# Attention on eight cores: statistics taken inside the projection loop, scores and value products issued in another order

## What is computed

```python
# attention: 16 heads of 64, latent 128, 32 "rope" columns a head
q = rms_norm((x @ Wq) per head, q_g)
kv = x @ Wkv                      # 128 latent columns
k = rms_norm((kv @ Wk) per head, k_g)      # 32 columns a head
v_c = (kv @ Wv) per head                   # 32 columns a head
scores = einsum('bhtr,bhsr->bhts', q[..., :ROPE], k) / sqrt(HD)
probs = softmax(where(causal, -inf, scores))
out = einsum('bhts,bhsd->bhtd', probs, v_c), padded to 64 columns a head
attn = out @ Wo
# linear layer: blocks of 32 of xn and of the weight rounded to a 6-bit grid
ffn = xd @ wd.T + bias
return x + attn + ffn
```

## Time and profile before

| what | value |
|---|---|
| median of 2 runs | 5157.03 us (5156.27 to 5157.78) |
| the profiled execution | 5152.05 us |
| its span, slowest core (7) | 5150.5 us |
| spans of the 8 cores | 5126.5 to 5150.5 us |
| PE busy | 3178.5 us (62%) |
| DVE busy | 1221.0 us (24%) |
| ACT busy | 603.1 us (12%) |
| DMA | 101.99 MB, mean 20 GB/s |

### The profile page before, as it was taken

How to read it: one execution, slowest core, us unless ns; L and a number is a source line. 1 busy time by engine, 2 the same in 40 slices (tenths; PEclk the granted TensorE clock), 3 DMA queues, 4 the chain that set the end, 5 groups by cost and what they waited for, 6 DMA issues and landing times.

```text
span 5150.5 us, 61902 instructions; the slowest of 8 cores (5126.5 to 5150.5 us)
## 1 busy us (share of the span) xinstructions
PE 3178.5 (62%) x26106; PEld 2348.7 (46%) x26106; DVE 1221.0 (24%) x2264; ACT 603.1 (12%) x587; POOL 85.2 (2%) x164
## 2 busy tenths in 40 slices
PE   0455577777411354667777776777776776763777
PEld 0333355555300121224666665465662664453777
DVE  7322211111377667621000000100002000113000
ACT  0000000000000000001333332133330332120000
POOL 0000000000000000000000000000000000001111
PEclk6555677777655667786877777687776887675998
DMA  4111200000000010000000000000000000000222
GB/s 121 53 37 37 66 9 13 13 13 13 13 17 16 12 33 17 33 25 1 1 1 1 1 1 1 1 1 1 1 1 0 1 1 1 17 22 5 62 65 63
DMA packets 50904, 101.99 MB, mean 20 GB/s; under 512 B 8582, under 2 KB 26822, under 8 KB 50632
## 3 DMA queue, kind: packets, MB, share of 16 engines
q1 hardware_dynamic: 45512, 89.50, 5.5%
q0 software_dynamic: 5120, 8.53, 0.7%
HBM read 81.09 MB, written 16.78 MB: 19 GB/s over the span
## 4 chain that ended last, share of the span: by engine, by line
PE 57%; DVE 20%; issue 11%; ACT 7%; DMA 3%; SPq 1%; DVEq 1%; POOL 0%; ACTq 0%; POOLq 0%
PE psA L151 31%; PE psB L151 21%; ACT arena L911 6%; PE psA L156 5%; DMA arena<-xown 2%; DVE arena L503 1%; SPq L144 1%; DVEq L108 1%; DVE arena L396 1%; DVE arena L394 1%; DVE arena L735 1%; DVE arena L595 1%; DMA arena<-arena 1%; DVE arena L858 1%; DVE arena L399 1%
## 5 line engine op out<-in xcount | busy, mean ns | idle before, releaser
L151 PE MATMUL psA<-arena 32*128 32x128 f32 (+5 forms) x15616 | 1625.5, 331 | 343.6 <-DVE arena L983 103.5
L151 PE MATMUL psB<-arena 128*64 128x128 f32 (+3 forms) x9814 | 1297.9, 384 | 671.0 <-ACT arena L911 504.2
L151 PEld LDWEIGHTS psA<-arena 32*128 32x128 f32 (+4 forms) x15616 | 1325.5, 225 | 672.6 <-issue 639.4
L151 PEld LDWEIGHTS psB<-arena 128*64 128x64 f32 (+3 forms) x9814 | 918.1, 188 | 996.3 <-issue 981.8
L156 PE MATMUL psA<-arena 128*128 128x128 f32 (+1 forms) x608 | 264.0, 434 | 909.5 <-DVE arena L384 460.8
L911 ACT ACTIVATE arena<-psA,arena 128x1024 f32<-128x1024 f32 x544 | 580.0, 1111 | 1587.1 <-PE psA L151 1587.1
L156 PEld LDWEIGHTS psA<-arena 128*128 128x128 f32 (+1 forms) x608 | 106.8, 176 | 1067.6 <-issue 1067.6
L943 DVE TENSOR_TENSOR arena<-psB,arena 128x1024 f32<-128x1024 f32 x24 | 29.4, 1225 | 1046.5 <-PE psB L151 1046.5
L939 DVE COPY arena<-psB 128x1024 f32<-128x1024 f32 x16 | 19.6, 1225 | 777.7 <-PE psB L151 777.7
L625 ACT ACTIVATE arena<-psB,arena 16x128 f32<-16x128 f32 x16 | 5.8, 360 | 1191.5 <-PE psB L151 1191.5
L820 ACT ACTIVATE arena<-psA,arena 16x1024 f32<-16x1024 f32 x4 | 4.4, 1107 | 1062.9 <-PE psA L151 1062.9
(11 more groups left out here) (84 smaller groups left out, 914.4 us busy)
## 6 DMA issues: line engine op xcount, KB each, us to landing
arena<-xb SPq DMA_DIRECT2D x64, 512.0 KB, 3.4
arena<-xown SPq DMA_DIRECT2D x48, 512.0 KB, 4.7
out<-arena SPq DMA_DIRECT2D x32, 256.0 KB, 2.3
arena<-out POOLq DMA_DIRECT2D x128, 64.0 KB, 2.7
out<-arena SPq DMA_DIRECT2D x128, 64.0 KB, 2.0
arena<-wq SPq DMA_DIRECT2D x8, 512.0 KB, 8.5
arena<-fw SPq DMA_DIRECT2D x8, 512.0 KB, 3.4
arena<-wop SPq DMA_DIRECT2D x8, 512.0 KB, 7.2
```

Source lines behind the costliest of these rows:

```text
L151: lambda e: e.matmul(out, lhsT, rhs, start=start, stop=stop, tile_position=tp, skip_group_check=skipg),
```

## The change

Two edits that share nothing. **In stage A** the separate statistics pass is gone: the projection loop now loads each tile once, into one of four buffers instead of two (`abufs`), and takes its sums and its mean and inverse root at once, on one column, before the projection of the same tile. **In stage D** the 16 score matmuls are issued bank by bank (r outside, j inside) instead of going round the banks, and the AV matmuls take first the eight heads whose probabilities are in the first exponential (0, 1, 4, 5, 8, 9, 12, 13), then the other eight.

```diff
--- before.py
+++ after.py
@@ -473,22 +473,44 @@
             t_cskv = dve(lambda e: e.tensor_copy(cskv(), bank(6, 0, LAT, 0, 1)),
                          waits=[tmm])
 
-            tuse = [None, None]
-            t_st = stats(w, dx, NT, tuse)
-            t_fin = stat_finish(w, NT, t_st)
-
-            tuse = [t_fin, t_fin]
+            abufs = [tmt(0), tmt(1), xet(0), xet(1)]
+            tuse4 = [None] * 4
             t_kv_prev = None
+            t_fin = None
             for it in range(NT):
-                bi = it % 2
-                t_l = dma("sync", tmt(bi)[:], dx[128 * it:128 * it + 128, :],
-                          waits=[tuse[bi]])
+                bi = it % 4
+                t_l = dma("sync", abufs[bi][:], dx[128 * it:128 * it + 128, :],
+                          waits=list(tuse4[bi] or ()))
+                t1 = dve(lambda e, it=it, bi=bi: e.reduce_sum(
+                    stc(0, it), abufs[bi][:], AX), waits=[t_l])
+                t2 = dve(lambda e, bi=bi: e.tensor_tensor(
+                    qs(3), abufs[bi][:], abufs[bi][:], OP.mult), waits=[t1])
+                t3 = dve(lambda e, it=it: e.tensor_reduce(
+                    stc(1, it), qs(3), AX, OP.add), waits=[t2])
+                tf = dve(lambda e, it=it: e.tensor_scalar(
+                    stc(2, it), stc(0, it), 1.0 / 1024, None, OP.mult),
+                    waits=[t3])
+                tf = dve(lambda e, it=it: e.tensor_tensor(
+                    qs(2, 0, 1), stc(2, it), stc(2, it), OP.mult), waits=[tf])
+                tf = dve(lambda e, it=it: e.scalar_tensor_tensor(
+                    qs(2, 64, 1), stc(1, it), 1.0 / 1024, qs(2, 0, 1),
+                    OP.mult, OP.subtract), waits=[tf])
+                tf = act(lambda e: e.activation(qs(2, 0, 1), qs(2, 64, 1),
+                                                AF.Ln, bias=epsln(), scale=1.0),
+                         waits=[tf, t_eps])
+                tf = act(lambda e, it=it: e.activation(stc(3, it), qs(2, 0, 1),
+                                                       AF.Exp, bias=zcol(),
+                                                       scale=-0.5),
+                         waits=[tf, t_z])
+                tf = dve(lambda e, it=it: e.tensor_scalar(
+                    stc(0, it), stc(2, it), -1.0, None, OP.mult), waits=[tf])
+                t_fin = tf
                 tpm = pet(bank(3, 0, 128, 0, 1), stc(0, it), idt(),
-                          waits=[t_fin, w.tok("dv")])
+                          waits=[tf, w.tok("dv")])
                 t_evm = dve(lambda e: e.tensor_copy(mrow(), bank(3, 0, 128, 0, 1)),
                             waits=[tpm])
                 tpa = pet(bank(6, 0, 128, 0, 1), stc(3, it), idt(),
-                          waits=[t_fin, w.tok("dv")])
+                          waits=[tf, w.tok("dv")])
                 t_eva = dve(lambda e: e.tensor_copy(arow(), bank(6, 0, 128, 0, 1)),
                             waits=[tpa])
                 tra = mm(bank(7, 0, 128), onesr(128), arow(), True, True,
@@ -496,10 +518,12 @@
                 t_ar = dve(lambda e: e.tensor_copy(areps(), bank(7, 0, 128)),
                            waits=[tra])
                 t_ev = []
+                pe_last = None
                 for ci in range(8):
                     tp = pet(bank(ci // 4, 128 * (ci % 4), 128),
-                             tmt(bi)[:, 128 * ci:128 * ci + 128], idt(),
+                             abufs[bi][:, 128 * ci:128 * ci + 128], idt(),
                              waits=[t_l, w.tok("dv")])
+                    pe_last = tp
                     t_ev.append(dve(lambda e, ci=ci: e.tensor_copy(
                         xfms(ci), bank(ci // 4, 128 * (ci % 4), 128)), waits=[tp]))
                 for ci in range(8):
@@ -512,7 +536,7 @@
                     kvf(128, 128 * it), bank(2, 0, 128),
                     areps()[0:LAT, :], OP.mult), waits=[tmm, t_ar])
                 t_kv_prev = t_kv
-                tuse[bi] = t_kv
+                tuse4[bi] = (t_kv, pe_last)
             t_kv_done = w.tok("dv")
 
             if stop_after == "A":
@@ -880,8 +904,10 @@
                         continue
                     av_started = {}
                     av_last = {}
+                    av_order = ([h for h in range(16) if h % 4 < 2] +
+                                [h for h in range(16) if h % 4 >= 2])
                     for st in range(lo, hi):
-                        for head in range(16):
+                        for head in av_order:
                             av_last[((head // 2) // 4, 64 * (head % 2))] = (st, head)
                     t_avmm = None
                     for st in range(lo, hi):
@@ -890,8 +916,9 @@
                         pcnt[0] += 1
                         t_exp = [None, None]
                         lastb = [None] * 4
-                        for h in range(16):
-                            r, j = h % 4, h // 4
+                        for r in range(4):
+                          for j in range(4):
+                            h = 4 * j + r
                             lastb[r] = mm(
                                 setap2(r, 128 * j, 128),
                                 khat(h // 4, 128 * (st - sup * spt), 128)[32 * r:32 * r + 32, :],
```

## The result

| | before | changed |
|---|---|---|
| median | 5152.49 us (10 runs, 5145.44 to 5197.6) | 4975.49 us (11 runs, 4970.83 to 5121.05) |
| profiled execution | 5152.05 us, span 5150.5 | 4973.29 us, span 4971.8 |
| ratio | | 0.9657, 95% interval 0.9625 to 0.9688 |

The changed kernel is faster by 177 us, where 457 were forecast. Single executions of any of these kernels are now and then some per cent longer; the ratios leave them out, so a ratio is not the quotient of two medians.

The account below looks back on a forecast made before the run. Attention's steps were taken as bound by a chain of waits, with more lost to the half clock. 5152 - 520 (stage D) + 64 (stage A) = 4696, median 4700 us; range 4630 to 5350, the forecast's own 4630 to 4780.

Parts of the forecast that it names:

- the AV order: Stage D steps: eight AV heads fill the second wait, saving 0.75 us a step; plain 4.55 us, masked 7.23, together -532.
- the half clock: Stage D: a few stretches after a slot begins run at reduced clock, so -520 us is taken instead of -532.
- stage A: Token tile loop: statistics moved into the projection pass cost +64 us, between +50 and +85, with a 20.3 us period.
- the chain: Stage A: the small statistics operations run once per tile, 32 times at 1.90 us, net +59 us.
- the clock of the kv matmuls: Stage A: longer TensorE idling may slow the nine kv matmuls per tile; up to 20 us, taken as 5.
- the cost of the score order: Stage D: the 16 scores issued bank by bank still take 1.24 us a step, not 3.74; the order changes nothing.
- rival 3: Stage D scores: TensorE reaches only two or three quarters; scores 1.9 to 2.4 us, 4730 to 4950; 0.17 shared with another rival.
- Rival 1: Stage D scores: matmuls start only after those ahead have started; 3.04 us a step, kernel slower at 5340 us; chance 0.17.
- rivals 1 and 2: Stage D scores queue: 5340 us with some overlap (0.17); with none and a sinking clock, 5600 or beyond 6300 (0.08).
- the clock: Stage D: shorter steps and less idling put all steps at the full clock, 1.00, instead of a mean of 0.75.

Follow-up runs that it names:

- the blocks of two: The changed kernel with scores issued two matmuls per row quarter, then two of the next, instead of bank by bank: 4702.58 us, ratio 0.9136.
- the filler: The changed kernel with two unread 128-row matmuls added per step between the scores and the first AV: 4918.23 us, ratio 0.9549.

## Why the prediction was right and wrong

**Right: the AV order.** Forecast 4.55 us a plain step and 7.23 a masked one, 1323 us for all; with the AV order alone 4.59 us, 7.3 and 1320 us, the whole kernel 4686 where 4700 stood. The wait was filled by six heads as worked out. What it saves is 1833 - 1320 = 513 us and not 532, since the windows of the earlier trace rows, 1855 us in sum, are 22 us too wide; the 12 us that the forecast took off for the half clock were not needed, and the two errors nearly cancel, which is luck.

**Right: stage A.** +64 forecast, +63 in the profiled executions with and without it. The terms hold too: 20.3 us a tile against 20.47, the chain 1.90 against 1.71 us. What is left over the 14.62 + 3.82 + 1.71 us is 0.3 us a tile, 10 us in all, where I put 5 on the clock of the kv matmuls; the shorter chain, 6 us, nearly makes up for it. That both edits add up was taken for granted; the runs of each alone show it.

**Wrong: the cost of the score order.** This is the step that failed: of 1.24 and 3.74 us a step for the 16 scores, the forecast took the first. The measured time is 2.82 us. The next quarter starts only when no more than three records of the one before it wait. In the earlier trace rows the four that start together pass over one waiting record in each quarter, three in all, and a reach of three explains them just as well as one of sixty does. The rows bound the reach from below, and I took it as unbounded. In kind this is rival 3, which put 1.9 to 2.4 us and 4730 to 4950 on it with a small chance; it was priced too low, and the time lies just above its end.

**Wrong: strict order.** Rival 1 rests on matmuls that start only when those ahead have started. By it only one record of each quarter would overlap the next quarter; the sixth record's start beside the fifth, with three of the first quarter still waiting, and the 1.29 us of the blocks of two speak against it. The Trainium skill, "TensorE: Matmul & The Clock Gate", Part 3, on packing small matmuls, states that order; here it does not hold. The depth of 64 that the same page gives for the queue is not the reach either: the 16 score matmuls of the bank order do not run side by side. Still, the rival's 3.04 us of scores were nearer to the measured 2.82 than the forecast's 1.24. What kept the kernel from becoming slower is above all the clock: rivals 1 and 2 divided by 0.75, and the steps were granted 0.93 to 0.96. (Two slips stand in the prediction: the page's order is the case of its first rival, not of the second, and 5.9 us at the half clock are 11.8, not 11.3.)

**Where the 268 us of the steps went** (1588 with both orders, 1320 with AV alone):

| term | working | us |
|---|---|---|
| longer plain step, full clock | 240 x (5.20 - 4.59) | 146 |
| longer masked step | 32 x (8.97 - 7.32) | 53 |
| the rest, clock below 1.00 | 268 - 146 - 53 | 69 |

The 7.32 us are a masked tile in the timeline with AV alone, 2467.91 to 2475.23. A count bears the rest out: 53 of the 240 plain steps are 1.4 us longer than the others of their kind, 74 us, and the filler gave back about 80. Of the 1.65 us that the scores are longer, a plain step shows only 0.6. The first exponential waits for banks 0 and 1 alone and starts 1.80 us after the first score (2682.38 to 2684.18), 1.31 in the round order (2707.24 to 2708.55); the other banks' scores run under it, where TensorE had nothing to do. That is 0.5 us; the other 0.1 is in the two exponentials, 2.22 us instead of 2.12. In a masked step the mask matmuls already lie there, and the whole 1.65 us shows.

**Wrong: the clock.** "I take the full clock for all steps" holds with the AV order alone (1.00) and not for the kernel that was forecast: 0.93 to 0.96, the 69 us of the table. The step came from the busy share of the earlier trace rows, and the runs deny that it decides: 69% busy went with 1.00 (AV alone), 94% with 0.95 (both orders), 88% with 0.80 (scores alone). What TensorE did ahead of these clocks differs. In the round order the 32-row matmuls run four at a time for 1.2 us; in bank order they fill 2.8 us with a quarter or two of the array at work. Matmuls of 128 rows added to either kernel brought the clock to 1.00. Which of these things the clock follows was not measured by itself.

## What to carry to other kernels

Where small matmuls share the array by rows, give neighbours in the program different row quarters, and as here different banks: runs of two in one quarter were nearly free, runs of four cost 1.65 us a step. To serve a consumer that needs half of the results first, try reordering the consumer's side alone first, as the AV order did: here it gave 289 us more than both orders together. Rows that show a mechanism at work bound only what they asked of it; if a change asks for more, keep the far end as a case with a real chance. And before shortening a wait on TensorE, ask what could fill it: the next step's scores gave 300 us, and even matmuls that nobody reads gave 6.5% through the clock.

## What the runs showed that was not expected

- Unread matmuls make the kernel before faster: 5152 to 4819 us, with the granted clock of its plain steps going to 1.00.
- TensorE starts a score matmul ahead of up to nine waiting records, if no more than three wait in one quarter (and bank). In the bank order record six starts within 0.02 us of record five, in another quarter, and every quarter starts 0.55 us after the last.
- A step whose TensorE is busy 94% of the time can have a lower clock (0.95) than one that is busy 69% (1.00).
